# Six attention layers: projections two tiles ahead moved ahead of the scores, and the orders of ScalarE, GpSimd and VectorE with them

## Chip, cores and metric

One core of a Trainium2 chip runs the whole program once. The metric is the device time in microseconds, lower is better. Five engines run their own instruction streams in order (TensorE for matmuls, VectorE, ScalarE, GpSimd, and SyncE, which issues transfers) and meet only at semaphores that the program names.

## The reference

The input is x of shape (4, 512, 128), float32: 4 sequences (batches) of 512 tokens, 128 features.

```
x = x + attention0(layernorm(x))           # 16 heads of 8, low-rank projections, rotary
x = x + stack(layernorm(x))                # 6 layers, below
x = x + attention1(layernorm(x))           # 16 heads of 8
x = x + experts(layernorm(x))              # top-1 of 16 experts, capacity 160

for i in range(6):                         # the stack
    y = shift_tokens(x)                    # second half of the features from the token before
    q, k, v = split(y @ Wqkv[i])           # 16 heads of 64
    q, k = l2norm(q) * qs, l2norm(k) * ks
    q, k = rotary(q) * scale, rotary(k) / scale
    a = softmax(8 * q k^T over a window of 32 and the one before)
    x = (a v) @ Wo[i] + x
    z = layernorm(shift_tokens(x)) * g + b
    a, gate = split(z @ W1[i] + b1)        # 341 and 341
    x = (a * gelu(gate)) @ W2[i] + b2 + x
```

The change is in the six layers of the stack alone.

## The kernel before

The stack is written as 24 iterations `it` (6 layers x 4 batches), each of 4 slots `i`, one for each tile of 128 tokens; T = 4 it + i counts the 96 tiles. `layer_slots` (its body is a hardware loop over layers) calls a function `slot` of each engine, and the order of calls in `slot` is the order in which that engine works; it is written out by hand. A slot is a stretch of a software pipeline: it has the scores and softmax of tile T, the preparation of the queries and keys of T+1, the projections of T+2 and the weighting of T-1. The feed-forward of a batch runs in between, one or two iterations later.

The life of a tile:

1. TensorE `project` (L859): 8 matmuls, two halves; half 0 is queries, half 1 is keys. ScalarE `take` (L1266) copies each half from PSUM to `raws`, and counts `l_raw`. ScalarE `squares` (L1274).
2. GpSimd `turn_swapped` (L580, L581): the half rotations, swapped halves times the sine table, for queries and keys together, in two operations, into `rotB`. It needs both halves of `raws`, and that both additions from `rotB` for the tile before have been made.
3. VectorE `square_sums` (L1563, L1564); ScalarE `guess` (L1280, L1283) makes a first value of the inverse root, GpSimd `inverse_root` (L589 to L592, 32 columns each) refines it.
4. VectorE `turn_plain` (L1569): times the cosine table; VectorE `add_queries` (L1574) and GpSimd `add_keys` (L597) add `rotB`; VectorE `scaled` (L1584) multiplies queries (half 0) and keys (half 1) by the inverse norms.
5. TensorE `turn_keys` (L870), `turn_queries` (L885) transpose; ScalarE `keys` (L1288), `queries` (L1292) copy; TensorE `scores` (masks L892, then 128 small matmuls L902).
6. VectorE `softmax`: maximum (L1590) and subtraction (L1595) from PSUM; ScalarE `exponentials` (L1296); VectorE `sums` (L1600, reciprocal L1605); GpSimd `normalise` (the division, L602); VectorE `turn_probs` (L1612), a transposition, in the next slot.
7. TensorE `weigh` (L923), in the next slot, into the PSUM banks of scores and queries; ScalarE `weighed` (L1305) copies; TensorE `turn_windows` (L915) waits for the first of these copies, ScalarE `windows` (L1310). TensorE `mix` (L933) folds in Wv Wo, 16 matmuls a slot in two pieces.

Beside these stands the feed-forward of an earlier iteration. TensorE's part is dealt out by `feed(j, l, i, point)` at four points of a slot: mean (L298), variance (L302), three gate products (L962), three plain ones (L970), the output (L976). ScalarE: `shift_ffn`, `ln_squares` (L314), `layer_root` (L318, L320), `gate` (L1327), `gelus` (L1333, L1334, between two loads of the function table). VectorE: `centre` (L306), `scale_norm` (L1640, L1644), `hidden` (L1650), `ffn_end` (L1655), `residual` (L1632). In slot i=2 of the last batch VectorE also makes the tables of the next layer (`tables`, L1619, L1623), and in two slots of a layer TensorE and ScalarE make its mixed weights (`weights` L945, `mixed_weights` L1339).

GpSimd's slot before is, in its own order: copy of the window edge (L610), `inverse_root` and `add_keys` for T+1, `normalise` for T, `turn_swapped` for T+2. VectorE's is: `square_sums` T+1, `turn_probs` T-1, `turn_plain` T+1, `add_queries` T+1, `softmax` T, `scaled` T+1 half 0, `sums` T, `scaled` T+1 half 1.

## Time and profile before

| | |
|---|---|
| time, median of 3 runs | 2735.58 us (2729.66 to 2739.02) |
| profiled execution | 2730.72 us, span 2728.9 us |
| TensorE (PE) busy | 2169.6 us, 80% |
| VectorE (DVE) busy | 1973.4 us, 72% |
| ScalarE (ACT) busy | 1509.5 us, 55% |
| GpSimd (POOL) busy | 1492.2 us, 55% |
| the 96 tiles of the stack | 428 to 2144 us |

Shares are over the whole span, with stages that have other limits; the stack is 63% of it. The granted clock of TensorE is given as a share of full speed. All spans of instructions are of one execution.

### The profile page before, as it was taken

The numbers are of one execution on the slowest core, as the hardware profiler recorded it, in microseconds if no ns is written. First come the engines' busy times: TensorE is split into PE (matmuls) and PEld (weight loads), VectorE is DVE, ScalarE is ACT, GpSimd is POOL, SyncE is SP. The second block draws the span as 40 slices with busy tenths as digits, with TensorE's granted clock in tenths as the row PEclk, the third lists the DMA queues.
The fourth block names the chain that finished last, engine by engine and source line by source line (L and its number), as shares of the span: only waits on it lengthen the run. The fifth ranks groups of instructions, "written<-read, shape, count | busy, mean of one in ns | idle before, by whom it ended". The sixth has DMA issues, their size and how long they took to land.

```text
span 2728.9 us, 53797 instructions
## 1 busy us (share of the span) xinstructions
PE 2169.6 (80%) x21684; PEld 1154.6 (42%) x21780; DVE 1973.4 (72%) x2087; ACT 1509.5 (55%) x1863; POOL 1492.2 (55%) x1031
## 2 busy tenths in 40 slices
PE   4768875888998989888889889889988756678734
PEld 1111123555555555555555555555555411111334
DVE  1766628888888888888888888888889426676211
ACT  2255564566676666666766676666766321455600
POOL 5500017777776776777776777777777234100033
PEclk7787897999999999999999999999999866897967
DMA  4100000000001000100010000000000001000133
GB/s 149 60 19 25 13 2 1 17 2 17 2 2 26 17 2 2 26 2 17 1 26 2 17 2 9 19 17 2 1 9 2 1 18 67 22 27 13 32 92 86
DMA packets 55828, 59.08 MB, mean 22 GB/s; under 512 B 13142, under 2 KB 45012, under 8 KB 55508
## 3 DMA queue, kind: packets, MB, share of 16 engines
q1 hardware_dynamic: 53444, 50.77, 6.1%
q0 software_dynamic: 2128, 4.72, 0.7%
q8 instruction: 182, 2.98, 0.5%
q14 instruction: 74, 0.61, 0.1%
HBM read 44.07 MB, written 11.01 MB: 20 GB/s over the span
## 4 chain that ended last, share of the span: by engine, by line
PE 36%; POOL 19%; DVE 17%; issue 16%; ACT 9%; DMA 2%; SPq 1%; POOLq 0%; DVEq 0%; ACTq 0%
PE bank L735 5%; PE bank L706 4%; PE bank L859 4%; DVE big L1463 4%; PE bank L923 4%; PE bank L933 4%; POOL big L580 3%; POOL big L597 3%; POOL big L581 3%; DVE big L1569 3%; POOL small L590 2%; ACT big L1180 2%; ACT pxs L1305 2%; PE bank L976 2%; DVE small L1563 2%
## 5 line engine op out<-in xcount | busy, mean ns | idle before, releaser
L1463 DVE TENSOR_REDUCE big<-bank 128x1 f32<-128x512 f32 x512 | 327.7, 685 | 199.3 <-PE bank L706 195.3
L602 POOL TENSOR_TENSOR sc<-sc,small 128x1024 f32<-128x1024 f32 x96 | 263.4, 2744 | 365.4 <-DVE small L1605 365.4
L859 PE MATMUL bank<-wqk,xs 128*128 128x512 f32 x768 | 359.2, 610 | 13.6 <-ACT xs L1261 8.3
L933 PE MATMUL bank<-pxs,mw 128*128 128x256 f32 x1536 | 366.2, 382 | 0.0
L1296 ACT ACTIVATE sc<-sc 128x1024 f32<-128x1024 f32 x96 | 101.5, 1057 | 464.0 <-DVE sc L1595 463.9
L933 PEld LDWEIGHTS bank<-pxs,mw 128*128 128x128 f32 x1536 | 291.1, 192 | 102.7 <-issue 71.9
L1180 ACT ACTIVATE big<-bank 128x1024 f32<-128x1024 f32 x256 | 250.2, 1026 | 140.1 <-PE bank L720 137.1
L1569 DVE TENSOR_TENSOR big<-big,rotCl 128x2048 f32<-128x2048 f32 x96 | 226.2, 2356 | 78.1 <-POOL big L581 78.1
L706 PE MATMUL bank<-pxs 48*128 48x512 bf16 x512 | 183.6, 439 | 117.1 <-DVE big L1463 74.0
L1563 DVE TENSOR_REDUCE small<-big 128x32 f32<-128x2048 f32 x96 | 219.0, 2281 | 39.5 <-ACT big L1274 30.2
L1584 DVE TENSOR_TENSOR big<-big,small 128x1024 f32<-128x1024 f32 x192 | 246.5, 1284 | 1.1 <-POOL small L592 1.1
L923 PE MATMUL bank<-sc,xnat 32*128 32x512 f32 x1536 | 202.7, 643 | 43.5 <-ACT big L1266 40.7
L580 POOL TENSOR_TENSOR big<-big,rotSl 128x1024 f32<-128x1024 f32 x96 | 227.6, 2371 | 8.4 <-ACT big L1266 8.2
L581 POOL TENSOR_TENSOR big<-big,rotSl 128x1024 f32<-128x1024 f32 x96 | 227.3, 2368 | 0.0
L597 POOL TENSOR_TENSOR big<-big 128x1024 f32<-128x1024 f32 x96 | 226.4, 2359 | 0.0
L859 PEld LDWEIGHTS bank<-wqk,xs 128*128 128x128 f32 x768 | 139.5, 191 | 164.6 <-issue 156.1
L1305 ACT ACTIVATE pxs<-bank 128x1024 f32<-128x1024 f32 x192 | 185.6, 1019 | 26.6 <-PE bank L923 23.1
L706 PEld LDWEIGHTS bank<-pxs 48*128 48x128 bf16 x512 | 40.4, 95 | 356.0 <-DVE big L1463 269.2
L1274 ACT ACTIVATE big<-big 128x2048 f32<-128x2048 f32 x96 | 183.3, 1910 | 11.5 <-DVE small L1564 1.1
L1266 ACT ACTIVATE big<-bank 128x1024 f32<-128x1024 f32 x192 | 184.8, 1011 | 5.2 <-PE bank L859 5.2
L720 PE MATMUL bank<-pxs 56*128 56x512 bf16 x512 | 118.5, 412 | 57.6 <-DMA pxs<-big 32.4
L902 PE MATMUL bank<-kbuf,qT 64*32 64x64 f32 x12288 | 145.5, 226 | 17.8 <-issue 14.3
(244 smaller groups left out, 3945.1 us busy)
## 6 DMA issues: line engine op xcount, KB each, us to landing
wqk<-in_L_ffn_Wqkv SPq DMA_DIRECT2D x12, 512.0 KB, 4.4
pxs<-part_rows SPq DMA_DIRECT2D x64, 96.0 KB
pxs<-part_rows SPq DMA_DIRECT2D x64, 64.0 KB
wqk<-in_L_ffn_w SPq DMA_DIRECT2D x16, 256.0 KB, 3.0
wvt<-in_wv_layers_t SPq DMA_DIRECT2D x6, 512.0 KB, 4.7
wol<-in_L_ffn_Wo SPq DMA_DIRECT2D x6, 512.0 KB, 5.8
part_rows<-big SPq DMA_DIRECT2D x24, 128.0 KB
part_rows<-sc SPq DMA_DIRECT2D x24, 128.0 KB
```

The source lines that it names most:

```text
L580: pool.tensor_tensor(r4[:, :, :, 0:h], q4[:, :, :, h:], tab[:, :, :, 0:h], ALU.mult).then_inc(l_rb, 1)
L581: pool.tensor_tensor(r4[:, :, :, h:], q4[:, :, :, 0:h], tab[:, :, :, h:], ALU.mult).then_inc(l_rb, 1)
L597: pool.tensor_tensor(raws(i)[:, INNER:], raws(i)[:, INNER:], rotB[:, INNER:], ALU.add).then_inc(l_ak, 1)
L602: pool.tensor_tensor(p3, p3, rden(i).unsqueeze(2).broadcast_to([P, LH, 64]), ALU.mult).then_inc(l_pn, 1)
L706: pe.matmul(bank[:, 4 + r, :], qst[64 * r:64 * r + MAX_ROW, b % 2, p, qt * P:(qt + 1) * P], kst[64 * r:64 * r + MAX_ROW, b % 2, p, :], sta ...
L859: m = pe.matmul(bank[:, 2 - 2 * half + c, :], xs[:, b % 2, WIN + i * P:WIN + (i + 1) * P], wqk[:, (2 * half + c) * 512:(2 * half + c + 1) ...
L923: m = pe.matmul(bank[:, (4, 5, 2, 3)[w], :], xnat[32 * w:32 * w + 32, i % 2, half, :], p4[32 * w:32 * w + 32, :, half, :], start=(half == ...
L933: m = pe.matmul(bank[:, 6, part * 2 * P:(part + 1) * 2 * P], mw[:, 2 * (a % 4) + s, a // 4, :], pxs[:, part, a, s, :], start=(a == 0 and s ...
L1180: act.activation(pT[:, u % 2, 2 * half:2 * half + 2, :], bank[:, q:q + 2, :], ACT.Exp).then_inc(a_p, 1)
L1463: dve.tensor_reduce(nm[:, qt, 2 * p + r:2 * p + r + 1], bank[:, 4 + r, :], AX.X, ALU.max, negate=True).then_inc(a_mx, 1)
L1563: ch.link(dve.tensor_reduce(ss, sq.rearrange("p (h d) -> p h d", d=LD), AX.X, ALU.add))
L1569: dve.tensor_tensor(r4, r4, rotCl[:, i % TILES, :].rearrange("p (a d) -> p a d", a=2).unsqueeze(2).broadcast_to([P, 2, LH, LD]), ALU.mult) ...
```

## The change

Only orders change, and the counts of the waits that follow from them; no operation is added, taken away or resized.

- TensorE: `project` of T+2 moves from behind the scores to ahead of them, keys first (half 1, then 0); `scores` moves ahead of the pieces of mixing and feed-forward; the points of `feed` shift (mean from point 2 to 1 of i=3, variance from point 3 of i=3 to point 0 of i=0, plain products and the output one point later).
- ScalarE: `take` (keys first) and `squares` of T+2 move ahead of `exponentials`; `gate` 2 and `gelus` move behind it; `layer_root` moves to the next slot, ahead of the exponent; `ln_squares` to the end of slot 3.
- GpSimd: `turn_swapped` of T+2 moves ahead of `normalise` of T.
- VectorE: `hidden` 1 from i=1 to i=2, `hidden` 2 behind the sums, `ffn_end` from i=2 to i=3, `scale_norm` and `centre` behind the sums.

```
--- before.py
+++ after.py
@@ -611,12 +611,12 @@
                 if ahead >= 1:
                     inverse_root(T + 1, (i + 1) % 2)
                     add_keys(T + 1, (i + 1) % 2)
-                normalise(T, i)
                 if ahead >= 2:
                     if b == BATCH - 1 and i == 2:
                         pool.wait_ge(l_tab, 3 * l + 6)
                         settle(pool)
                     turn_swapped(T + 2, (i + 2) % TILES)
+                normalise(T, i)
 
             pool.wait_ge(l_tab, 3)
             turn_swapped(0, 0)
@@ -847,7 +847,7 @@
             def project(it, l, b, i, half):
 
                 T = it * TILES + i
-                if i == 0 and half == 0:
+                if i == 0 and half == 1:
                     pe.wait_ge(l_xs, 2 * it + 2)
                 if i == 0 and b == 0:
                     pe.wait_ge((ld_q, ld_k)[half], 16 * l + 16)
@@ -873,7 +873,7 @@
 
             def turn_queries(T, l, b, i):
                 if isinstance(T, int) and T < 2:
-                    pe.wait_ge(l_raw, 2 * T + 3)
+                    pe.wait_ge(l_raw, 2 * T + 4)
                 else:
                     pe.wait_ge(l_pc, 2 * T - 2)
                 if b == 0 and i == 3:
@@ -978,19 +978,19 @@
 
             def feed(j, l, i, point):
 
-                if i == 3 and point == 2:
+                if i == 3 and point == 1:
                     mean_of(j)
-                if i == 3 and point == 3:
+                if i == 0 and point == 0:
                     ln_var_of(pe, LAYER0 + j, 7)
                 if i == 0 and point == 3:
                     gate(j, l, 0)
                 if i == 1 and point <= 1:
                     gate(j, l, 1 + point)
-                if i == 1 and point >= 2:
-                    plain(j, point - 2)
-                if i == 2 and point == 0:
-                    plain(j, 2)
-                if i == 2 and point == 2:
+                if i == 1 and point == 2:
+                    plain(j, 0)
+                if i == 2 and point <= 1:
+                    plain(j, 1 + point)
+                if i == 2 and point == 3:
                     ffn_out(j)
 
             def mixing(it, l, b, i, j):
@@ -1019,26 +1019,26 @@
                 fl = l - (1 if (b < (1 if i == 3 else 2)) else 0)
                 turn_keys(T, i, ahead)
                 turn_queries(T, l, b, i)
+                if ahead >= 2:
+                    k = i + 2
+                    for half in (1, 0):
+                        project(it + k // TILES, l + (1 if b == BATCH - 1 and k >= TILES else 0), (b + k // TILES) % BATCH, k % TILES, half)
+                scores(T, it, i)
                 if feeds:
                     feed(fed, fl, i, 0)
                 if mixes:
                     mixing(it, l, b, i, 0)
                 if feeds:
                     feed(fed, fl, i, 1)
-                scores(T, it, i)
-                if ahead >= 2:
-                    k = i + 2
-                    for half in range(2):
-                        project(it + k // TILES, l + (1 if b == BATCH - 1 and k >= TILES else 0), (b + k // TILES) % BATCH, k % TILES, half)
+                if mixes:
+                    mixing(it, l, b, i, 1)
                 if feeds:
                     feed(fed, fl, i, 2)
-                if mixes:
-                    mixing(it, l, b, i, 1)
                 if not (first and i == 0):
                     pe.wait_ge(l_pt, T)
                     pe.wait_ge(l_e, T + 1)
                     if ahead >= 2:
-                        pe.wait_ge(l_raw, 2 * T + 5)
+                        pe.wait_ge(l_raw, 2 * T + 6)
                     else:
                         pe.wait_ge(l_qe, T + 1)
                     settle(pe)
@@ -1053,9 +1053,9 @@
             pe.wait_ge(zeros_set, 2)
             pe.wait_ge(step_done, LAYER0 + 1)
             for T in range(2):
-                for half in range(2):
+                for half in (1, 0):
                     if T == 1:
-                        pe.wait_ge(l_raw, 1 + half)
+                        pe.wait_ge(l_raw, 2 - half)
                     project(0, 0, 0, T, half)
             layer_slots(pe, slot)
             N = DEPTH * BATCH * TILES
@@ -1262,7 +1262,7 @@
 
             def take(T, i, half):
 
-                act.wait_ge(l_qk, 2 * T + half + 1)
+                act.wait_ge(l_qk, 2 * T + 2 - half)
                 act.activation(raws(i)[:, half * INNER:(half + 1) * INNER],
                                bank[:, 2 - 2 * half:4 - 2 * half, :].rearrange("p a t -> p (a t)"), ACT.Copy).then_inc(l_raw, 1)
 
@@ -1348,26 +1348,26 @@
                 queries(T, i)
                 if ahead >= 1:
                     guess(T + 1, (i + 1) % 2)
+                if ahead >= 2:
+                    take(T + 2, i % 2, 1)
+                    take(T + 2, i % 2, 0)
+                    squares(T + 2, i % 2)
                 if i == 3 and not first:
                     shift_ffn(it - 1, (b - 1) % BATCH)
+                if i == 0 and feeds:
+                    layer_root(it - 2)
                 if i == 1 and feeds:
                     gate(it - 2, 1)
+                exponentials(T, i)
+                if i == 1 and feeds:
                     gate(it - 2, 2)
                     gelus(it - 2)
-                exponentials(T, i)
-                if ahead >= 2:
-                    take(T + 2, i % 2, 0)
-                    take(T + 2, i % 2, 1)
-                if i == 3 and not first:
-                    ln_squares(act, LAYER0 + it - 1)
-                if ahead >= 2:
-                    squares(T + 2, i % 2)
                 if not (first and i == 0):
                     for half in range(2):
                         weighed(T - 1, it if i else it - 1, (i - 1) % TILES, half)
                 windows(T, i)
                 if i == 3 and not first:
-                    layer_root(it - 1)
+                    ln_squares(act, LAYER0 + it - 1)
                 if i == 0 and feeds:
                     gate(it - 2, 0)
                 if i == 0 and not (isinstance(it, int) and it == LAST):
@@ -1386,7 +1386,7 @@
             act.wait_ge(step_done, LAYER0 + 1)
             shifted(0, 0)
             for T in range(2):
-                for half in range(2):
+                for half in (1, 0):
                     take(T, T, half)
                 squares(T, T)
             guess(0, 0)
@@ -1394,6 +1394,7 @@
             N = DEPTH * BATCH * TILES
             for half in range(2):
                 weighed(N - 1, LAST, TILES - 1, half)
+            layer_root(LAST - 1)
             for n in range(3):
                 gate(LAST - 1, n)
             gelus(LAST - 1)
@@ -1670,23 +1671,24 @@
                     add_queries(T + 1, (i + 1) % 2)
                 if b == BATCH - 1 and i == 2 and more:
                     tables(l + 1)
+                softmax(T, i)
+                if i == 2 and feeds:
+                    hidden(it - 2, 1)
+                if i == 3 and feeds:
+                    ffn_end(it - 2, (b - 2) % BATCH)
+                if ahead >= 1:
+                    scaled(T + 1, (i + 1) % 2, 0)
+                sums(T, i)
+                if i == 0 and feeds:
+                    scale_norm(it - 2, l - (1 if b < 2 else 0))
                 if i == 2 and feeds:
                     hidden(it - 2, 2)
-                softmax(T, i)
-                if i == 0 and feeds:
-                    scale_norm(it - 2, l - (1 if b < 2 else 0))
-                if ahead >= 1:
-                    scaled(T + 1, (i + 1) % 2, 0)
                 if i == 3 and not first:
                     centre(it - 1)
-                sums(T, i)
                 if ahead >= 1:
                     scaled(T + 1, (i + 1) % 2, 1)
                 if i == 1 and feeds:
                     hidden(it - 2, 0)
-                    hidden(it - 2, 1)
-                if i == 2 and feeds:
-                    ffn_end(it - 2, (b - 2) % BATCH)
                 if i == 2 and not first:
                     residual(it - 1, (b - 1) % BATCH)
```

## Rows read from the trace of the kernel before

**Rows 1.** Busy time by engine (us, x instructions), granted clock, transfers: one window of the stack.
```profile
1100.00:1500.00 400.00, 355.99 (x4285) 216.65 (x4305) 351.64 (x293) 259.02 (x318) 297.84 (x193) 0.98 0.05 13
```

**Rows 2.** One line's instructions, the subtraction: min/median/max ns, first and last start.
```profile
L1595 DVE TENSOR_TENSOR sc<-bank,small x96: 1224/1225/1226, 428.1 to 2143.5; 128x1024 f32<-128x1024 f32 x96
```

**Rows 3.** Groups of lines, 560 to 2000 us: busy us, mean ns | idle before, releaser.
```profile
L602 POOL TENSOR_TENSOR sc<-sc,small 128x1024 f32<-128x1024 f32 x79 | 217.5, 2753 | 299.7 <-DVE small L1605 299.7
...
L1569 DVE TENSOR_TENSOR big<-big,rotCl 128x2048 f32<-128x2048 f32 x80 | 188.4, 2354 | 65.3 <-POOL big L581 65.3
```

**Rows 4.** Timeline of an ordinary iteration, slots 1 to 3: start us, length us, what.
```profile
1455.89 1.28 ACT L1333 ACT_TABLE_LOAD   x1
...
1458.77 1.28 ACT L1335 ACT_TABLE_LOAD   x1
1459.84 1.22 DVE L1595 TENSOR_TENSOR sc<-bank,small 128x1024 f32<-128x1024 f32 x1 [0.18 <-DVE small L1590]
...
1467.96 1.04 PE L870 MATMUL bank<-ident,big 128*128 128x128 f32 x8
...
1469.12 1.03 ACT L1288 ACTIVATE kbuf<-bank 128x1024 f32<-128x1024 f32 x1 [0.29 <-PE bank L870]
...
1471.27 1.23 DVE L1612 STREAM_TRANSPOSE sc<-sc 128x1024 f32<-128x1024 f32 x1
...
1472.43 2.24 DVE L1569 TENSOR_TENSOR big<-big,rotCl 128x2048 f32<-128x2048 f32 x1
...
1472.81 1.48 PE L902 MATMUL bank<-kbuf,qT 64*32 64x64 f32 x128
1474.22 3.70 PE L859 MATMUL bank<-wqk,xs 128*128 128x512 f32 x8
1474.71 1.22 DVE L1574 TENSOR_TENSOR big<-big 128x1024 f32<-128x1024 f32 x1
...
1476.51 1.21 DVE L1590 TENSOR_REDUCE small<-bank 128x16 f32<-128x1024 f32 x1
...
1477.90 1.23 DVE L1595 TENSOR_TENSOR sc<-bank,small 128x1024 f32<-128x1024 f32 x1 [0.18 <-DVE small L1590]
...
1481.64 0.25 DVE L1605 RECIPROCAL small<-small 128x16 f32<-128x16 f32 x1 [0.17 <-DVE small L1600]
1481.81 1.16 DVE L1584 TENSOR_TENSOR big<-big,small 128x1024 f32<-128x1024 f32 x1
1481.97 2.75 POOL L602 TENSOR_TENSOR sc<-sc,small 128x1024 f32<-128x1024 f32 x1 [3.31 <-DVE small L1605]
...
1484.27 2.29 DVE L1563 TENSOR_REDUCE small<-big 128x32 f32<-128x2048 f32 x1
...
1484.69 2.38 POOL L580 TENSOR_TENSOR big<-big,rotSl 128x1024 f32<-128x1024 f32 x1
...
1487.01 2.39 POOL L581 TENSOR_TENSOR big<-big,rotSl 128x1024 f32<-128x1024 f32 x1
...
1489.43 2.33 DVE L1569 TENSOR_TENSOR big<-big,rotCl 128x2048 f32<-128x2048 f32 x1 [1.17 <-POOL big L581]
...
1493.40 2.35 POOL L597 TENSOR_TENSOR big<-big 128x1024 f32<-128x1024 f32 x1
...
1495.47 1.36 DVE L1584 TENSOR_TENSOR big<-big,small 128x1024 f32<-128x1024 f32 x1
...
1529.77 1.23 DVE L1595 TENSOR_TENSOR sc<-bank,small 128x1024 f32<-128x1024 f32 x1 [0.17 <-DVE small L1590]
```

**Rows 5.** Single lines, min/median/max ns (L602 over the whole run, the others 560 to 2000 us).
```profile
L602 POOL TENSOR_TENSOR sc<-sc,small x96: 1901/2752/2757, 432.2 to 2147.6; 128x1024 f32<-128x1024 f32 x96
...
L1564 DVE TENSOR_SCALAR small<-small x79: 475/1399/2152, 575.5 to 1994.0; 128x32 f32<-128x32 f32 x79
...
L1640 DVE TENSOR_TENSOR sqn<-xc,hT x20: 681/1159/1168, 567.6 to 1949.7; 128x512 f32<-128x512 f32 x20
...
L1644 DVE TENSOR_SCALAR xc<-sqn,lb x20: 545/547/550, 569.0 to 1951.1; 128x512 f32<-128x512 f32 x20
```

More of the change, by code:

```diff
@@ L849, in project @@
                 T = it * TILES + i
-                if i == 0 and half == 0:
+                if i == 0 and half == 1:
                     pe.wait_ge(l_xs, 2 * it + 2)
@@ L1021, in slot @@
                 turn_queries(T, l, b, i)
+                if ahead >= 2:
+                    k = i + 2
+                    for half in (1, 0):
+                        project(it + k // TILES, l + (1 if b == BATCH - 1 and k >= TILES else 0), (b + k // TILES) % BATCH, k % TILES, half)
+                scores(T, it, i)
                 if feeds:
@@ L1027, in slot @@
                     feed(fed, fl, i, 1)
-                scores(T, it, i)
-                if ahead >= 2:
-                    k = i + 2
-                    for half in range(2):
-                        project(it + k // TILES, l + (1 if b == BATCH - 1 and k >= TILES else 0), (b + k // TILES) % BATCH, k % TILES, half)
+                if mixes:
+                    mixing(it, l, b, i, 1)
                 if feeds:
                     feed(fed, fl, i, 2)
-                if mixes:
-                    mixing(it, l, b, i, 1)
                 if not (first and i == 0):
@@ L1055, in _ @@
             for T in range(2):
-                for half in range(2):
+                for half in (1, 0):
                     if T == 1:
-                        pe.wait_ge(l_raw, 1 + half)
+                        pe.wait_ge(l_raw, 2 - half)
                     project(0, 0, 0, T, half)
@@ L1350, in slot @@
                     guess(T + 1, (i + 1) % 2)
+                if ahead >= 2:
+                    take(T + 2, i % 2, 1)
+                    take(T + 2, i % 2, 0)
+                    squares(T + 2, i % 2)
                 if i == 3 and not first:
                     shift_ffn(it - 1, (b - 1) % BATCH)
+                if i == 0 and feeds:
+                    layer_root(it - 2)
                 if i == 1 and feeds:
                     gate(it - 2, 1)
+                exponentials(T, i)
+                if i == 1 and feeds:
                     gate(it - 2, 2)
                     gelus(it - 2)
-                exponentials(T, i)
-                if ahead >= 2:
-                    take(T + 2, i % 2, 0)
-                    take(T + 2, i % 2, 1)
-                if i == 3 and not first:
-                    ln_squares(act, LAYER0 + it - 1)
-                if ahead >= 2:
-                    squares(T + 2, i % 2)
                 if not (first and i == 0):
@@ L1388, in _ @@
             for T in range(2):
-                for half in range(2):
+                for half in (1, 0):
                     take(T, T, half)
@@ L1672, in slot @@
                     tables(l + 1)
+                softmax(T, i)
+                if i == 2 and feeds:
+                    hidden(it - 2, 1)
+                if i == 3 and feeds:
+                    ffn_end(it - 2, (b - 2) % BATCH)
+                if ahead >= 1:
+                    scaled(T + 1, (i + 1) % 2, 0)
+                sums(T, i)
+                if i == 0 and feeds:
+                    scale_norm(it - 2, l - (1 if b < 2 else 0))
                 if i == 2 and feeds:
                     hidden(it - 2, 2)
-                softmax(T, i)
-                if i == 0 and feeds:
-                    scale_norm(it - 2, l - (1 if b < 2 else 0))
-                if ahead >= 1:
-                    scaled(T + 1, (i + 1) % 2, 0)
                 if i == 3 and not first:
                     centre(it - 1)
-                sums(T, i)
                 if ahead >= 1:
@@ L1686, in slot @@
                     hidden(it - 2, 0)
-                    hidden(it - 2, 1)
-                if i == 2 and feeds:
-                    ffn_end(it - 2, (b - 2) % BATCH)
                 if i == 2 and not first:
```

25 lines of the change are left out of this document (13 added, 12 removed).

## The prediction

> **What bounds the kernel now.** I read the table of windows first. In 400 us of the layer stage TensorE is busy 356, VectorE 352, GpSimd 298, and TensorE's granted clock is 0.98 of full speed, that is its 2.4 GHz level [rows 1]. The 96 maximum subtractions of the layer stage start from 428.1 to 2143.5 us [rows 2]: 1715.4 / 95 = 18.06 us a tile, against 13.5 to 16.1 us of work on one of these engines (their share of the 400 us times 18.06). So no engine is full; a loop of waits sets the period. The groups of lines name its two ends: GpSimd's division L602 waits 299.7 us for VectorE's reciprocal, and VectorE's cosine product L1569 waits 65.3 us for GpSimd's second half rotation L581 [rows 3]. The timeline shows the loop for slot i=2 [rows 4]: subtraction 1477.90, reciprocal 1481.64, division 1481.97, half rotations 1484.69 and 1487.01, cosine product 1489.43. All four slots of this ordinary iteration take 1529.77 - 1459.84 = 69.9 us.
>
> The rows show a second thing, on which my sum rests. GpSimd and VectorE exclude each other in some pairs. L602 takes 1.90 us at its fastest and 2.75 at the median [rows 5]; the long ones start 0.16 us behind a scaling L1584, which ends 1.00 us later (1481.81 to 1482.97, division to 1484.72) [rows 4]. In the other direction L1584 at 1495.47 takes 1.36 instead of 1.16, ending 1.1 us after the key addition L597 ends (1493.40 + 2.35 = 1495.75) [rows 4]. L1640, two inputs in SBUF as well, takes 0.68 or 1.16 [rows 5]. The 32-column L1564 takes 0.48 to 2.15, and at 1484.27 + 2.29 it waits for the half rotation that ends at 1487.07 [rows 4, 5]. VectorE's reductions, its transposition and the subtraction from PSUM run beside GpSimd at their own length. So L1569, L1574, both L1584, L1640 and L1564 ("port operations" below) take turns with every GpSimd operation, and whoever waits at an end goes next.
>
> **The change, part by part.** Count from t = 0, the end of VectorE's second scaling (L1584) for tile T, in the new slot.
>
> VectorE: the reduction L1563 and L1564 need 2.7 us, the transposition L1612 1.2, L1569 2.3, L1574 1.15 (starts 1484.27, 1471.27, 1472.43, 1474.71 and what follows them, [rows 4]). The half rotations for T+1 were made in the slot before, so the 1.2 us wait before L1569 is gone: VectorE is free at 7.3. Unblocked, its starts add up to 13.7 us for a plain tile.
>
> TensorE: the projections (3.5 us from start to start; the row says 3.70) now stand between the transpositions and the scores. They need ScalarE's copy of the keys, which in the rows ends 2.2 us after the transpositions start (1467.96, 1469.12 + 1.03). Before, mixing products stood there. So: projections 2.3 to 5.9, masks and scores (L902 1.48 us and 0.3 before it) to 7.7, maximum at 7.8, subtraction from 9.2 to 10.4 (1476.51 to 1477.90 is 1.4 us) [rows 4]. TensorE waits some 0.2 us and VectorE 0.5; both small. The matmuls themselves are the same number at the same clock, hence no term.
>
> ScalarE: copies of the raw projections and the squares (1.9 + 1.9 us) lie in the idle stretch ahead of the exponent, free. But in slot i=1 two table loads and two Gelus, 1455.89 to 1460.05 = 4.2 us [rows 4], move behind the exponent, where the weighted copies L1305 are queued, then turn_windows and the next transpositions. Exponent to 11.7, gate copy 12.4, Gelus 16.6, L1305 17.7, transpositions of the next tile at about 18.0. That bounds slot 1 from transposition to transposition, against 18.2 now.
>
> GpSimd: the small steps of the inverse root are held up by L1569 and L1574 until 7.4, end near 8.0; the key addition L597 runs to 10.4; then two half rotations of 2.35 each, then the division. The reordering puts 7 us of GpSimd work in one piece exactly where VectorE wants two port operations. The first scaling arrives at 10.4, a tie with the end of L597; if it loses, it waits until 12.8 and ends at 13.9. The sums take until 15.5; the second half rotation, held until 13.9, ends at 16.1; the second scaling follows to 17.2. So a plain slot is 17.2 us, not 13.7, and nearly what it is now (about 17): the wait before L1569 has gone into the two scalings. I charge 1.1 us for an L1584 that waits, its own length, and 2.2 for a half rotation that was held.
>
> The Trainium skill ("SBUF — State Buffer", section "Who interferes with whom") says that the pair shared by VectorE and GpSimd is an exclusive lock and that issue order, not shape, decides who blocks. By it the new order of issue pays at both scalings, and a held GpSimd operation should keep its full length: with 1.90 instead of the 1.75 that the row shows, each iteration would be 0.5 us longer. I stay with the row.
>
> VectorE's extras: `hidden(1)` (i=2) and `ffn_end` (i=3) stand ahead of a scaling that waits anyway, free. `hidden(0)` and `residual` cost their 0.7, mostly absorbed by the 0.5 us of slack at the scores. `scale_norm` in i=0 now stands behind the sums, at 15.5: L1640 waits for the second half rotation until 16.6 or so, the division is next, L1644 comes behind it and the second scaling last, near 20.0. L1644 (0.547 us for 512 columns, faster than L1640's 0.68) [rows 5] is not seen beside GpSimd here. The nearest row, the other tensor_scalar L1564, does wait. Bound from below: it doesn't wait, slot 0 is 19.6. I take it that it waits: 20.0. It also makes gate 0 late on TensorE (17 to 19 instead of behind the softmax), with turn_windows and the key transpositions queued behind it.
>
> The same Trainium skill section says that `tensor_scalar` can enter a mode that takes the shared pair; by that L1644 waits and slot 0 is 20.0, otherwise 19.6. No row here decides it.
>
> Sum for an ordinary iteration. Slot 0: 20.0. Slots 1 and 2 together 36.0: whether the scaling wins its tie in slot 1 (15.6, then 20.5 since the transposition comes late and the division gets in first) or loses it (17.8 and 17.8), the pair is the same within 0.5. Slot 3: 17.3 (ffn_end hidden, mean on TensorE waits for it but finishes in time). 20.0 + 36.0 + 17.3 = 73.3, less 69.9 = +3.4 us. Of the 24 iterations 22 carry feed-forward work: 22 x 3.4 = +75 us. The first two, the layer changes (tables, mixed weights) and the tail (`layer_root` moved) I cost at nothing: the same operations in the same waits, bounds -10 and +15. The profiled execution took 2730.7 us (span 2728.9), giving 2806; the median of the runs is 2735.6, giving 2810. Mis-sized arrivals of 0.1 us decide turns worth 2 us, so the sum has wide bounds: with L1644 unblocked and all ties lost 72.4 (+55 us, 2790), own range 2770 to 2840.
>
> **The rivals.**
> A, the order does what it says: the wait goes and the scalings find gaps. Then the first scaling gets in ahead of the first half rotation and the second between the two; such a slot is 14.9 and the next, whose division comes late, 17.8, mean 16.3; with 0.5 for extras 16.8 x 4 = 67.2, -2.7 x 22 = -59 us: 2676. For it: the tie at 10.4 is within 0.1 us. Against: two slots have 0.7 us of work ahead of the scaling, and it decides only if the subtraction ends before L597 in most slots.
> B, the loop changes its place but not its length: 69.9 stays, 2736. A mixture of A and the forecast.
> C, a cascade: in slot 0 the tie is lost, gate 0 comes after 19, ScalarE's `shifted` and then the key copy come 1.3 us late, each later slot's scores are late, and in slot 3 the division gets in before the second scaling (21.0). 20.05 + 17.9 + 17.85 + 21.05 = 76.8, +6.9 x 22 = +152: 2887.
>
> **How the numbers follow.** Forecast 0.48, A 0.24, B 0.11, C 0.17. 0.3% (8 us, about what a measurement of this kernel can tell from no change) is 0.37 us an iteration, little against the ties, so B is small. The range 2680 to 2885 leaves out about half of A and half of C, 0.2. Faster 0.24, same 0.11, slower 0.65.
>
> **What would show it.** Right: the wait of L1569 for L581 is gone; L1584's mean rises from 1.26 to over 1.8 us; L602 waits little for L1605 except in slot 0; L1640 starts behind L1605 and is long; maximum L1590 waits for L902 in most slots. Wrong: L1584 stays near 1.3 (then A), or starts of L1595 four slots apart fall under 69 us; or TensorE's late gate 0 makes the key copies late and they run to 76 (C). Above all a wrong order of turns at the tie would break the sum.

## The result, and the profile after

The changed kernel takes 2833.2 us (median of 4, 2822.5 to 2841.1) beside 2737.3 us (median of 4) for the kernel before: ratio 1.0352, 95% interval 1.0303 to 1.0401, slower by some 96 us. The profiled execution of the changed kernel has a span of 2839.3 us. The 96 tiles of the stack take the time: the subtractions of the maximum (L1596 now; VectorE's lines have moved down by one) start from 437.1 to 2251.9 us, 1814.8 / 95 = 19.10 us a tile instead of 18.06 [rows 2].

The page of the changed kernel, busy time and chain. The chain is the work that ended last, followed back from the end. TensorE's share of it is 52%; it was 36% before, when GpSimd had 19%. GpSimd has 2% left.
```profile
PE 2212.9 (78%) x21684; PEld 1184.8 (42%) x21780; DVE 2017.3 (71%) x2087; ACT 1539.3 (54%) x1863; POOL 1486.0 (52%) x1031
...
PE 52%; DVE 22%; ACT 11%; issue 9%; POOL 2%; DMA 2%; SPq 1%; DVEq 0%; ACTq 0%; POOLq 0%
```

Groups of lines of the changed kernel, 560 to 2060 us (busy us, mean ns | idle before, releaser), first VectorE, then GpSimd.
```profile
L1585 DVE TENSOR_TENSOR big<-big,small 128x1024 f32<-128x1024 f32 x156 | 299.7, 1921 | 0.0
...
L1570 DVE TENSOR_TENSOR big<-big,rotCl 128x2048 f32<-128x2048 f32 x78 | 176.1, 2258 | 0.0
...
L1591 DVE TENSOR_REDUCE small<-bank 128x16 f32<-128x1024 f32 x77 | 94.3, 1225 | 187.5 <-PE bank L902 187.5
L1645 DVE TENSOR_SCALAR xc<-sqn,lb 128x512 f32<-128x512 f32 x20 | 37.2, 1861 | 4.1 <-DVE sqn L1641 4.1
...
L581 POOL TENSOR_TENSOR big<-big,rotSl 128x1024 f32<-128x1024 f32 x78 | 237.4, 3044 | 0.0
L602 POOL TENSOR_TENSOR sc<-sc,small 128x1024 f32<-128x1024 f32 x78 | 205.5, 2635 | 62.7 <-DVE small L1606 62.7
```
These answer to [rows 3, 5] and to two lines of the kernel before, 560 to 2000 us:
```profile
L1584 DVE TENSOR_TENSOR big<-big,small 128x1024 f32<-128x1024 f32 x158 | 198.8, 1258 | 0.0
L1590 DVE TENSOR_REDUCE small<-bank 128x16 f32<-128x1024 f32 x79 | 96.1, 1217 | 15.6 <-PE bank L902 15.5
```
The wait of the cosine product for the half rotation is gone, 65.3 us to 0.0, as forecast. The scalings L1585 are longer instead: 1.92 us where the group took 1.26. L1645 takes 1.86 instead of 0.55: a tensor_scalar with per-partition scalars does wait for GpSimd. And a wait that was nearly nothing (15.6 us) is now VectorE's largest: 187.5 us in which the maximum L1591 waits for the scores, 2.4 us a tile.

Timeline of the changed kernel, from slot 0 through slot 1 (start us, length us, what), beside [rows 4].
```profile
1586.76 1.85 DVE L1645 TENSOR_SCALAR xc<-sqn,lb 128x512 f32<-128x512 f32 x1 [0.19 <-DVE sqn L1641]
1588.53 1.21 DVE L1585 TENSOR_TENSOR big<-big,small 128x1024 f32<-128x1024 f32 x1
1588.67 2.08 PE L962 MATMUL bank<-xc,w 128*128 128x512 f32 x2 [3.20 <-DVE xc L1645]
...
1590.96 1.91 PE L870 MATMUL bank<-ident,big 128*128 128x128 f32 x8
...
1594.43 3.89 PE L859 MATMUL bank<-wqk,xs 128*128 128x512 f32 x8
...
1600.20 1.23 DVE L1591 TENSOR_REDUCE small<-bank 128x16 f32<-128x1024 f32 x1 [3.23 <-PE bank L902]
...
1601.60 1.22 DVE L1596 TENSOR_TENSOR sc<-bank,small 128x1024 f32<-128x1024 f32 x1 [0.18 <-DVE small L1591]
...
1602.74 1.24 DVE L1585 TENSOR_TENSOR big<-big,small 128x1024 f32<-128x1024 f32 x1
...
1602.86 3.34 POOL L581 TENSOR_TENSOR big<-big,rotSl 128x1024 f32<-128x1024 f32 x1
...
1605.52 1.76 DVE L1585 TENSOR_TENSOR big<-big,small 128x1024 f32<-128x1024 f32 x1
1606.15 2.89 POOL L602 TENSOR_TENSOR sc<-sc,small 128x1024 f32<-128x1024 f32 x1
...
1610.17 1.04 PE L870 MATMUL bank<-ident,big 128*128 128x128 f32 x8
...
1616.46 1.48 PE L902 MATMUL bank<-kbuf,qT 64*32 64x64 f32 x128
...
1617.99 1.22 DVE L1591 TENSOR_REDUCE small<-bank 128x16 f32<-128x1024 f32 x1 [1.49 <-PE bank L902]
...
1619.38 1.23 DVE L1596 TENSOR_TENSOR sc<-bank,small 128x1024 f32<-128x1024 f32 x1 [0.17 <-DVE small L1591]
```
See two things. The turns at the port are as described: the second scaling, started at 1605.52 while the half rotation L581 was running, ends at 1607.28, which is 1.08 us (about its own length) behind the end of L581 at 1606.20; and L602, held, takes 2.89. But the second scaling of slot 1 ends at 1607.3, and the key transpositions of the next tile start only at 1610.2. They wait for TensorE's own queue, in which the product ahead of them waits for ScalarE's weighted copy. From their start the next subtraction follows by 1619.38 - 1610.17 = 9.2 us, with no slack: over the tiles from 560 to 1960 us this distance is 9.22 us at the least and 9.28 at the median; behind slot 0 it is 10.4 to 10.6, and 11.6 at the most. In the kernel before it runs from 7.3 to 14.9, because there finished scores waited until VectorE came (1.8 us at the median). So in the changed kernel a chain through TensorE sets the slots: subtraction, weighting, weighted copy, transpositions, key copy, projections, scores, subtraction. It does so in every slot 1 and 2. At the end of slots 0 and 3 the transpositions start within 0.2 us of the second scaling in 10 of 40 cases, and there VectorE sets them.

The four slots from 1580.47 on take 21.1, 17.8, 18.8 and 18.8 us, 76.4 together. This is an iteration of batch 3, in which VectorE also makes the tables of the next layer, and the 69.9 us of [rows 4] are one of the shortest iterations (batch 2): the two don't compare. Means of the 21 iterations from the third to the last but one, us from subtraction to subtraction:

| | batch 0 | batch 1 | batch 2 | batch 3 | all |
|---|---|---|---|---|---|
| before | 72.6 | 72.9 | 70.7 | 74.5 | 72.6 |
| changed | 78.9 | 79.4 | 75.8 | 75.8 | 77.4 |

That is +4.8 us an iteration, and 21 x 4.83 = 101 us, the whole difference (the ends of the stack are 2 us shorter). By slot, 0 to 3, the means were 18.4, 19.3, 16.5 and 18.3 us and are 20.8, 17.8, 19.3 and 19.5. Slot 0 loses 2.4, slot 2 loses 2.7 and slot 3 loses 1.2. Slot 1 is 1.6 us shorter, and two thirds of that are batch 3's: its 22.4 us with the tables are now 17.8, since VectorE makes the tables where it would wait for the scores.

### The profile page after: what moved, and what is told of

Same layout as the page of the kernel before. It is cut to its first block, busy times and chain, and to the rows that moved or that the text cites. A ratio compares the mean times of both kernels' runs of the same rounds, so it can differ in the third digit from the quotient of the medians.

```text
span 2839.3 us, 53797 instructions
## 1 busy us (share of the span) xinstructions
PE 2212.9 (78%) x21684; PEld 1184.8 (42%) x21780; DVE 2017.3 (71%) x2087; ACT 1539.3 (54%) x1863; POOL 1486.0 (52%) x1031
## 4 chain that ended last, share of the span: by engine, by line
PE 52%; DVE 22%; ACT 11%; issue 9%; POOL 2%; DMA 2%; SPq 1%; DVEq 0%; ACTq 0%; POOLq 0%
PE bank L859 12%; DVE big L1585 6%; PE bank L735 5%; PE bank L902 5%; PE bank L706 4%; DVE big L1464 4%; PE bank L933 3%; DVE small L1591 3%; PE bank L962 3%; PE bank L870 3%; ACT kbuf L1288 3%; PE bank L976 2%; PE bank L923 2%; DVE small L1601 2%; ACT big L1180 2%
## 5 line engine op out<-in xcount | busy, mean ns | idle before, releaser
L1585 DVE TENSOR_TENSOR big<-big,small 128x1024 f32<-128x1024 f32 x192 | 376.4, 1961 | 1.1 <-POOL small L592 1.1
L1180 ACT ACTIVATE big<-bank 128x1024 f32<-128x1024 f32 x256 | 250.0, 1026 | 144.0 <-PE bank L720 141.7
L602 POOL TENSOR_TENSOR sc<-sc,small 128x1024 f32<-128x1024 f32 x96 | 253.8, 2643 | 88.1 <-DVE small L1606 88.1
L581 POOL TENSOR_TENSOR big<-big,rotSl 128x1024 f32<-128x1024 f32 x96 | 292.5, 3047 | 0.0
L1591 DVE TENSOR_REDUCE small<-bank 128x16 f32<-128x1024 f32 x96 | 117.6, 1225 | 227.3 <-PE bank L902 227.3
L706 PE MATMUL bank<-pxs 48*128 48x512 bf16 x512 | 189.8, 454 | 114.2 <-DVE big L1464 70.3
L1266 ACT ACTIVATE big<-bank 128x1024 f32<-128x1024 f32 x192 | 196.7, 1025 | 128.7 <-PE bank L859 128.6
L610 POOL COPY kbuf<-kbuf 128x256 f32<-128x256 f32 x72 | 95.3, 1324 | 282.7 <-ACT kbuf L1288 282.7
L580 POOL TENSOR_TENSOR big<-big,rotSl 128x1024 f32<-128x1024 f32 x96 | 228.8, 2383 | 25.2 <-POOL big L597 16.1
L1564 DVE TENSOR_REDUCE small<-big 128x32 f32<-128x2048 f32 x96 | 218.2, 2273 | 13.6 <-ACT big L1274 11.9
L1570 DVE TENSOR_TENSOR big<-big,rotCl 128x2048 f32<-128x2048 f32 x96 | 217.1, 2262 | 0.0
L923 PE MATMUL bank<-sc,xnat 32*128 32x512 f32 x1536 | 193.7, 618 | 6.3 <-DVE sc L1596 5.5
L589 POOL TENSOR_TENSOR small<-small 128x32 f32<-128x32 f32 x96 | 99.6, 1037 | 144.6 <-ACT small L1283 144.6
```

Source lines behind the costliest of these rows:

```text
L580: pool.tensor_tensor(r4[:, :, :, 0:h], q4[:, :, :, h:], tab[:, :, :, 0:h], ALU.mult).then_inc(l_rb, 1)
L581: pool.tensor_tensor(r4[:, :, :, h:], q4[:, :, :, 0:h], tab[:, :, :, h:], ALU.mult).then_inc(l_rb, 1)
L602: pool.tensor_tensor(p3, p3, rden(i).unsqueeze(2).broadcast_to([P, LH, 64]), ALU.mult).then_inc(l_pn, 1)
L706: pe.matmul(bank[:, 4 + r, :], qst[64 * r:64 * r + MAX_ROW, b % 2, p, qt * P:(qt + 1) * P], kst[64 * r:64 * r + MAX_ROW, b % 2, p, :], sta ...
L923: m = pe.matmul(bank[:, (4, 5, 2, 3)[w], :], xnat[32 * w:32 * w + 32, i % 2, half, :], p4[32 * w:32 * w + 32, :, half, :], start=(half == ...
L1180: act.activation(pT[:, u % 2, 2 * half:2 * half + 2, :], bank[:, q:q + 2, :], ACT.Exp).then_inc(a_p, 1)
```

## Experiments

Each is timed beside the kernel before; the ratio is to that kernel, and intervals are 95%. Slot lengths are those of the profiled execution.

**GpSimd's order undone in the changed kernel.**
```
                     inverse_root(T + 1, (i + 1) % 2)
                     add_keys(T + 1, (i + 1) % 2)
+                normalise(T, i)
                 if ahead >= 2:
...
                     turn_swapped(T + 2, (i + 2) % TILES)
-                normalise(T, i)
```


> The changed kernel with one thing undone: GpSimd's slot again divides tile T (L602) ahead of the half rotations of T+2. Theory (turns at the shared port): the 7 us block of GpSimd work in front of VectorE's two scalings is broken up by the wait for the reciprocal, L1585's mean falls from 1.92 to about 1.3 us, and the time falls by 80 to 110 us, to 2720 to 2755. Rival (TensorE's order: projections ahead of the scores make the softmax late): GpSimd's order matters little, L1591 still waits some 2 us a tile for the scores and the time stays above 2800.

2829.5 us, ratio 1.0346 (1.0302 to 1.0389): no different from the whole change. Timeline there, from the subtraction of slot 2 to that of slot 3:
```profile
1612.25 1.23 DVE L1596 TENSOR_TENSOR sc<-bank,small 128x1024 f32<-128x1024 f32 x1 [0.18 <-DVE small L1591]
...
1617.77 2.12 DVE L1585 TENSOR_TENSOR big<-big,small 128x1024 f32<-128x1024 f32 x1
...
1621.76 1.03 PE L870 MATMUL bank<-ident,big 128*128 128x128 f32 x8
...
1630.99 1.23 DVE L1596 TENSOR_TENSOR sc<-bank,small 128x1024 f32<-128x1024 f32 x1 [0.18 <-DVE small L1591]
```
The second scaling is over at 1619.9, 1.9 us ahead of the transpositions, and the next subtraction is again 9.2 us behind them. So in this slot the scalings aren't what TensorE waits for. The theory that the order of GpSimd makes the loss falls here. But the edit is a weak test of the port itself: L1585's mean fell from 1.92 to 1.70 us, not to the 1.3 expected, and at the end of slot 0, in each of 20 iterations, the key transpositions start 0.06 to 0.15 us behind the second scaling, so there VectorE sets the pace.
```profile
L1585 DVE TENSOR_TENSOR big<-big,small 128x1024 f32<-128x1024 f32 x157 | 266.2, 1696 | 0.0
```

**GpSimd's order alone**, the same edit the other way round in the kernel before.

> The kernel before with GpSimd's part of the change alone: half rotations of T+2 ahead of the division of T. The raw copies are still behind the exponent, so the rotations wait for them and the division waits behind the rotations. Theory (port): VectorE's transposition L1612 now waits for a division that ends near 16.8 us after the cosine product; a slot takes some 18 us where it took 16.4 to 17.2: +80 to +130 us, 2815 to 2870. Rival (TensorE's order is what costs): within 20 us of 2737.

2764.6 us, ratio 1.0133 (1.0087 to 1.0180), +32 us where 80 to 130 was expected. Waits of GpSimd and ScalarE there, 800 to 1900 us (total us, times, longest):
```profile
ACT sc L1296 <- DVE sc L1595: 305.9, 48, 11.2
POOL big L580 <- ACT big L1266: 214.5, 59, 7.2
```
The rotations wait for raw copies that ScalarE makes only behind the exponent. The move has a price by itself, a third of the whole; taken out of the changed kernel (the run above) it gives nothing back, so it doesn't add to the others.

**Shorter half rotations in the changed kernel**, 2 of 16 heads, so the other columns of the rotation are stale and the result is another one.
```
-pool.tensor_tensor(r4[:, :, :, 0:h], q4[:, :, :, h:], tab[:, :, :, 0:h], ALU.mult)
+pool.tensor_tensor(r4[:, :, 0:2, 0:h], q4[:, :, 0:2, h:], tab[:, :, 0:2, 0:h], ALU.mult)
```
(and the same for the other half)

> The changed kernel in which GpSimd's two half rotations work on 2 of the 16 heads only (the other columns of the result are stale, so the output is not the reference's). Same order, same instructions, about 4 us less GpSimd work a tile, and no long operation between the two scalings. Theory (port): L1585's mean falls to 1.2 to 1.4 us, slots fall to what TensorE and ScalarE allow, 16 to 17.8 us; the time falls by 90 to 180 us, to 2650 to 2740. Rival (TensorE's order): GpSimd isn't on the path, the time stays at 2800 to 2835.

2747.4 us, ratio 1.0067 (1.0043 to 1.0091). 86 us less, just short of the 90 to 180 expected; L1585's mean fell to 1.41 us. The maximum still waits 157.6 us for the scores:
```profile
DVE small L1591 <- PE bank L902: 157.6, 59, 6.1
```

**The same cut in the kernel before** (control).

> Control: the kernel before with GpSimd's half rotations on 2 of 16 heads (output not the reference's). Theory: the loop of the kernel before runs through these two operations, 4 us of each 16.4 to 18.2 us slot, so slots fall until TensorE (16 us busy a tile) binds; 2590 to 2670. With the same cut the changed kernel only came to 2747; the difference is what the change costs on TensorE's side alone, 80 to 150 us. Rival (TensorE already bounds the kernel before): 2700 to 2735.

2651.0 us, ratio 0.9704 (0.9667 to 0.9742). The cut takes 82 us from the order before and 86 us from the changed one; with it the changed order is still 2747 - 2651 = 96 us slower, as much as without. So the changed order loses 96 us even where GpSimd has hardly any rotation to do. That the two savings are equal is chance, though. The slots show it, means of 21 iterations in us:

| | slot 0 | slot 1 | slot 2 | slot 3 | four |
|---|---|---|---|---|---|
| before | 18.4 | 19.3 | 16.5 | 18.3 | 72.6 |
| before, rotations cut | 17.9 | 18.5 | 15.8 | 17.3 | 69.5 |
| changed | 20.8 | 17.8 | 19.3 | 19.5 | 77.4 |
| changed, rotations cut | 18.3 | 17.8 | 19.0 | 18.9 | 74.0 |

In the kernel before every slot gains 0.5 to 0.9 us. In the changed kernel slot 0 gains 2.6, slots 1 and 2 gain 0.0 and 0.2, and slot 3 gains 0.6. This is the reading that separates the causes: the port and GpSimd hold slot 0, where L1645 and gate 0 stand behind the half rotations; 4 us less of GpSimd work does nothing for slots 1 and 2, which are the chain's. What is left of the loss under the cut lies in slots 2 and 3 (+3.3 and +1.6 us).

**Scores ahead of the projections again, in the changed kernel.** In `slot` of TensorE the call of `scores(T, it, i)` stands ahead of the block with `project`.

> The changed kernel with TensorE's scores of T ahead of the projections of T+2 again, the rest as changed. Scores are ready 3.5 us earlier, so VectorE's subtraction ends at about 10.0 instead of 10.4 to 12 us into the slot and the first scaling gets its turn ahead of the first half rotation (they start at 10.4). Theory (port): the tie is won in plain slots, L1585's mean falls to about 1.5, time 2740 to 2790. Rival (only how late the scores are counts, port irrelevant): VectorE's wait for scores, 2.4 us a tile, goes in full, and the time falls below 2700.

2941.6 us, ratio 1.0777 (1.0731 to 1.0822): both theories wrong, 108 us slower than the whole change. Waits there, 800 to 1900 us:
```profile
ACT big L1266 <- PE bank L859: 210.3, 106, 5.6
DVE small L1601 <- ACT sc L1296: 163.0, 41, 5.2
```
ScalarE's raw copies stand ahead of the exponent in the changed order. With the projections late they wait (210 us), and the exponent and VectorE's sums wait behind them (163 us). Projections and raw copies must move together.

**Projections alone moved in the kernel before**, ahead of feed-forward, mixing and scores; the raw copies stay behind the exponent.

> The kernel before with one move: TensorE's projections of T+2 directly behind the transpositions of T, ahead of the first pieces of feed-forward and mixing and of the scores. ScalarE, VectorE and GpSimd as before. Theory (TensorE's chain from transposition to scores becomes as long as the loop through GpSimd): the scores end 9.5 to 11.3 us behind the second scaling where VectorE comes for them at 9.9, so slots 1 and 2 lose 1.4 and 0.5 us: +1.5 to 2.5 us an iteration, 2765 to 2795. Rival (the early projections are harmless, the loss comes from the feed-forward placement and the port): 2727 to 2750.

3100.4 us, ratio 1.1339 (1.1309 to 1.1369). The direction was right and the size far off (2765 to 2795 expected). Waits there, 900 to 1900 us:
```profile
DVE small L1590 <- PE bank L902: 189.0, 43, 7.4
...
PEld bank L859 <- ACT qT L1292: 87.3, 46, 2.9
PE bank L923 <- ACT big L1266: 84.2, 42, 2.9
```
With queries first, the projections wait for both of ScalarE's copies (2.9 us at the longest), and the weighting waits for raw copies behind an exponent that is itself behind the late scores. Scores, subtraction, exponent, raw copies, weighting, transpositions, projections and again scores have become one serial loop; its median slots are 24.1, 21.3, 19.3 and 22.1 us.

**The main moves of TensorE and ScalarE without the rest**: as the last, but keys first, with raw copies and squares ahead of the exponent; feed-forward pieces, Gelus and GpSimd as before.

> The kernel before with the moves that the change is named after on TensorE and ScalarE, keys first, raw copies and squares ahead of the exponent, but with the feed-forward pieces, the first mixing piece ahead of the scores and GpSimd's order all as before. Theory (feed-forward had to be moved with them, so its new placement is no loss of its own): scores end at 9.5 to 12.5 us, slot 1 has its Gelus ahead of the exponent and takes 20 us or more; 2840 to 2920, worse than the whole change. It is well under the 3100 of e8_projections_alone, since the raw copies no longer come behind the exponent. Rival (the new places of the feed-forward are the loss): 2740 to 2800.

2854.9 us, ratio 1.0452 (1.0412 to 1.0492), as expected: worse than the whole change. The main moves alone lose more than the whole change, 122 us, and the other moves (the new places of the feed-forward on TensorE and VectorE, the Gelus behind the exponent and GpSimd's order together) win back about 1%: 1.0452 against 1.0352.

**Gate 2 and the Gelus ahead of the exponent again, in the changed kernel.** `gate(it - 2, 2)` and `gelus(it - 2)` of slot 1 go ahead of `exponentials(T, i)`.

> The changed kernel with gate 2 and the Gelus back ahead of the exponent in slot 1. With the scores ahead of the feed-forward products, gates 1 and 2 come late on TensorE, so the 4.2 us of Gelus and table loads end some 6 us behind the subtraction. Theory (this move was forced by the other one, and is no part of the loss): the exponent, the sums and the second scaling of slot 1 are 5 us late, slot 1 goes from 17.8 to 20 to 21 us, +45 to +70 us, 2875 to 2905. Rival (Gelus behind the exponent are what makes the weighted copies and the next tile's transpositions late, and cost the time): slot 1 falls, the time drops under 2815.

2919.6 us, ratio 1.0683 (1.0649 to 1.0717): +86 us. Slot 1 goes from 17.8 to 21.7 us; both are more than expected (20 to 21 us, +45 to +70). The theory holds in kind: this move was forced by the other and is no loss of its own.

**scale_norm back ahead of the first scaling, in the changed kernel.**
```
                 softmax(T, i)
+                if i == 0 and feeds:
+                    scale_norm(it - 2, l - (1 if b < 2 else 0))
...
                 sums(T, i)
-                if i == 0 and feeds:
-                    scale_norm(it - 2, l - (1 if b < 2 else 0))
```


> The changed kernel with scale_norm (L1641, L1645) back between the softmax and the first scaling in slot 0; the rest as changed. Theory (late gate 0): in slot 0 of the changed kernel TensorE waits up to 5 us for L1645 before gate 0, and turn_windows and the key transpositions stand behind it; with the norm earlier that wait goes, slot 0 falls from 20.9 to about 19 us, the iteration by 1.5 to 2: -30 to -45 us, 2790 to 2805. Rival (the operations at the port only change places): the first scaling and the sums become late instead, slot 0 stays at 20 to 21 and the time at 2815 to 2840.

2797.2 us, ratio 1.0221 (1.0186 to 1.0256): -36 us. Waits of TensorE for L1645, 800 to 1900 us, first the changed kernel, then this one:
```profile
PE bank L962 <- DVE xc L1645: 50.0, 15, 4.4
```
```profile
PE bank L962 <- DVE xc L1645: 4.4, 10, 0.7
```
Slot 0 falls from 21.0 to 19.6 us at the median. The late gate 0 is a part of the loss by itself. With it gone, the key transpositions at the end of slot 0 start 0.06 to 0.15 us behind the second scaling in each of 20 iterations: now VectorE sets that slot.

**With it the mean product of slot 3 one point later** (point 2 instead of 1).

> The changed kernel with scale_norm back ahead of the first scaling (as in e3_scale_norm_back) and the mean product of slot 3 at point 2 instead of 1. Theory (TensorE's chain is one of two loops, and what lengthens it are products that wait for VectorE with the key transpositions queued behind them): the wait of L298 for ffn_end, 1.3 to 1.9 us in slot 3, goes too; 10 to 30 us below e3's 2797, 2767 to 2787. Rival (the loop through the port sets slot 3): same as e3 within 8 us.

2802.4 us, ratio 1.0257 (1.0216 to 1.0298): the rival, nothing gained. The wait of L298 for ffn_end is gone and slot 3 is 0.8 us shorter in the mean (19.3 to 18.5), but in slot 0 the second scaling ends 0.5 us later behind the subtraction (8.9 to 9.5 us), and that slot is 0.7 us longer (19.4 to 20.1), with which the gain is given back.

**That version with the short rotations** (again another result).

> e11_norm_back_mean_late with the short half rotations as well (output not the reference's): neither the port nor late feed-forward products hold the changed order of TensorE. Theory: what is left is TensorE's own chain, transpositions, wait for the key copy, projections, scores, mixing, weighting, wait for the weighted copy: some 68.5 us an iteration where the changed kernel with short rotations had 72.3; 2690 to 2720. Rival (the two late products only hid behind each other and the chain is as long without them): 2740 to 2750 as in e5_short_rotations.

2715.1 us, ratio 0.9929 (0.9905 to 0.9952). 32 us under the changed kernel with the same cut, and still 64 us over the kernel before with it (2651.0). With port and late products eased, slots 1 and 2 stay at 17.8 and 18.7 us at the median and each subtraction still follows its transpositions by 9.3 us at the median. So of the 96 us by which the two orders differ under the cut, 64 are left that neither late product explains. By slot, against the kernel before with the cut, they are -0.8, -0.7, +3.3 and +1.1 us: slot 2 above all. The port isn't wholly out of it (L1585's mean is 1.39 us here, 1.21 in the kernel before with the cut).

**A try at a better version: centre out of the loop, in the kernel before.**
```
                 if ahead >= 1:
                     scaled(T + 1, (i + 1) % 2, 1)
+                if i == 3 and not first:
+                    centre(it - 1)
```
(taken away ahead of `sums`; `ln_squares` goes to the end of slot 3, the variance product and `layer_root` to slot 0)

> An attempt at a better version: the kernel before with centre (L306) moved from ahead of the sums to behind the second scaling in slot 3, the squares of the layer norm to the end of that slot on ScalarE, the variance product to slot 0 point 0 and layer_root ahead of slot 0's exponent. Theory: in the kernel before, everything VectorE does between the subtraction and the reciprocal is in the loop through GpSimd's division and half rotations; centre's 0.68 us is moved to where VectorE waits 1.2 us for L581. -0.6 us for 22 iterations: 2720 to 2730. Rival: VectorE's wait there is used up already by the tile's own reductions, or the late layer_root delays the exponent in slot 0: 2735 to 2750.

2734.5 us, ratio 1.0004 (0.9989 to 1.0020): no difference, where 2720 to 2730 was expected. Slot 3 is 0.6 us shorter in batches 2 and 3 (17.2 to 16.7 and 17.5 to 16.8 us), and slots 2 and 3 of batch 0, where the mixed weights are made, give it back (16.9 to 17.7 and 18.7 to 19.8). No version with the right output beats the kernel before.

## Why the prediction came out as it did

The time, 2833 against 2810 forecast and 2737 before, lies in the range and near the forecast: +96 against +75. The steps behind it are less good than the time.

Right, and shown by the trace: the wait of the cosine product goes; the pieces at the port take turns, and L1585's mean rises to 1.92 ("over 1.8"); a half rotation that was held runs for 2.22 us behind the end of the scaling (1603.98 to 1606.20), as charged; L1645 waits, gate 0 is late (3.2 us in the timeline) and its undoing gives 36 us back; the maximum waits for the scores in every slot; the Gelus had to move. Slot 1 is 17.8 us at the median in every version with TensorE's new order that has them behind the exponent, with the half rotations long or short, which fits the bound of about 18.0 from ScalarE's paragraph; that the sum had 17.8 there from the turns at the port is luck. The Trainium skill ("SBUF — State Buffer", section "Who interferes with whom") lists tensor_scalar among the operations that can take the shared pair. L1645's 1.86 us agrees; my sum had taken that side from L1564.

Wrong: the step "a plain slot is 17.2 us ... the wait before L1569 has gone into the two scalings", that is the claim that GpSimd's block of work sets the slot. The scalings do become longer, but undoing GpSimd's order changes nothing, and cutting its rotations leaves slots 1 and 2 as long as they were. What sets them is the chain that the prediction priced in its paragraph on TensorE and called small ("TensorE waits some 0.2 us and VectorE 0.5; both small"). That paragraph sized the way from the transpositions to the subtraction well, 9.2 us and 9.2 measured, but started it at the end of the second scaling. The transpositions in fact start where TensorE's queue lets them: 2.5 us after the second scaling in slot 1, 2.6 in slot 2, 1.6 in slot 3 and 1.1 in slot 0 (medians). This was to be seen before: there the medians are 2.2, 2.7, 2.0 and 0.8. From there the projections (3.7 us of the 9.2) now lie between them and the scores, where the kernel before had a mixing piece and often a feed-forward product, and then the time in which finished scores waited for VectorE. VectorE's wait for the scores was forecast as 0.5 us and is 2.4.

That a plain slot came near is luck. Forecast were 8.0 us from the subtraction to the end of the second scaling, nothing to the transpositions and 9.2 to the next subtraction, 17.2; slots 1 and 2 have 6.0 and 7.0 at the median, then 2.5 and 2.6, then 9.2. The port was charged 1 to 2 us too much, and TensorE's queue at nothing.

The multiplication by 22 is luck too. The 69.9 us are an iteration of batch 2, where the mean of the 21 iterations is 72.6. Batch 2 costs 5.1 us and not the 3.4 forecast, batches 0 and 1 cost 6.4 and 6.5. Batch 3 costs 1.3, because the changed order hides the tables: the layer changes that were put at nothing give back 4.6 us in slot 1 each time.

One term was put at nothing with a wrong reason: "The matmuls themselves are the same number at the same clock, hence no term." The clock isn't the same, as the last section shows.

Slot by slot: 0 was forecast at 20.0 us and is 20.8 in the mean; 1 and 2 together at 36.0, and are 37.0; 3 at 17.3, and is 19.5 (18.0 in batch 2). In slot 3 ffn_end, behind the softmax, makes the mean product wait (20.2 us in 14 waits, 800 to 1900 us).

Of the rivals, A (the scalings find gaps) didn't happen. C, the cascade, did in part: its late key copy is there (the 9.2 us are 10.4 to 10.6 behind slot 0, in part because the clock is low there), and +4.8 us an iteration lies between the forecast's +3.4 and its +6.9.

What stays open. How much the port adds when TensorE's chain is the longer loop: GpSimd's order alone costs 32 us in the kernel before and about nothing in the changed one, and a kernel with the port free and nothing else changed wasn't run, since only the rotations were cut. And why slot 2 loses most: the change also moves one plain product (1.0 to 1.1 us) from slot 1 into it, and TensorE is busy there for 18.1 of 19.3 us from transpositions to transpositions (17.3 of 19.8 before). The order from transpositions to scores and this load weren't separated.

## What to carry to other kernels

When a piece of work is moved ahead of another on an in-order engine, write down that engine's own cycle (from an instruction to the same one of the next tile, waits for copies included) before pricing the wait that goes away: here a 1.2 us wait was taken out of one loop, and 3.7 us of projections put into another. Start that cycle where the trace shows the first instruction start, not where its input is ready. A product that is early for its reader is as late as possible for what it was put ahead of; matmuls that nobody waits for belong behind the ones on which the softmax hangs. To see which of two loops binds, make the same cut in both kernels, and read it by slot: 82 and 86 us in total looked like one common cause, but in one kernel they came off all slots and in the other off slot 0 for the most part. And before multiplying the difference of one iteration, check that it is as long as the mean: 4 x 18.06 = 72.2 us stood in the rows beside the 69.9.

## What the runs showed of the hardware that I had not expected

TensorE's clock pays for such waits a second time. Windows of the changed kernel (busy us of PE, PEld, DVE, ACT, POOL, then the granted clock, and transfers): the end of slot 0 before the wait, the 6 us behind gate 0, and what follows.
```profile
1580.00:1585.50 5.50, 5.47 (x33) 3.50 (x31) 5.14 (x6) 2.56 (x4) 5.33 (x3) 1.00 0.00 0
1588.60:1594.60 6.00, 5.93 (x21) 4.55 (x22) 5.90 (x6) 3.12 (x5) 0.06 (x1) 0.50 0.00 0
1594.60:1600.00 5.40, 5.35 (x137) 2.97 (x138) 2.34 (x2) 4.01 (x6) 4.64 (x6) 0.98 0.09 14
```
After TensorE had stood still for 3.2 us its granted clock was 0.50, the 1.2 GHz level, for 6 us. Gate 0 took 2.08 us instead of 1.13, and each set of eight transpositions 1.91 instead of 1.04: 2.7 us lost on top of the wait. In the 21 iterations the granted clock is 0.91 in slot 0 and 1.00 in slots 1 and 2. With the rotations cut it is 1.00 in slot 0 as well, so a part of the 2.6 us that slot 0 gains there is the clock's. Over 1500 us of the stack it is 0.96 on average where it was 0.98 (560 to 1990 us). In all, TensorE is busy for 2212.9 us with the same number of matmuls that took 2169.6: 43 us more, of which the part on the path wasn't measured.
```profile
560.00:2060.00 1500.00, 1281.15 (x15023) 785.15 (x15098) 1269.67 (x1025) 945.48 (x1134) 1043.18 (x677) 0.96 0.03 10
```
The copy of the window edge, GpSimd's L610, 256 columns with one input, takes 0.40 us at its fastest and 1.53 at the median beside VectorE's cosine product, so one input on GpSimd's side is enough to have to take turns:
```profile
L610 POOL COPY kbuf<-kbuf x58: 396/1532/2516, 567.5 to 2039.8; 128x256 f32<-128x256 f32 x58
```
